# A decoder's second cross attention: the experts' weighing behind the next period's second maximum, the scattered transfers in one group

## The reference, cut to what matters

```python
# cross attention, 16 heads of 16 channels, without a mask
q, k, v = heads(x @ Wq.T + bq), heads(ctx @ Wk.T + bk), heads(ctx @ Wv.T + bv)
probs = softmax(q @ k.T / sqrt(16))
x = layernorm(x + (probs @ v) @ Wo.T + bo)

# routing: 32 experts, 4 for each token, at most C places in each
scores = sigmoid(X @ gate_w.T)
_, idx = top_k(scores + bias, 4)
w = take_along_axis(scores, idx)
w = w / clip(sum(w), 1e-12)
pos = place of this choice among all tokens' choices of the same expert   # a running count
row idx*C + pos of the experts' input = X (dropped where pos >= C)
# later: the expert's output row times w, summed over the 4 choices
```

## Time and profile before

| | us |
|---|---|
| median of 3 runs | 2905.83 |
| lowest and highest | 2905.07, 2911.41 |
| the profiled execution | 2889.48 |
| its span on the core | 2887.5 |
| of it xattn1, about | 2237 to 2684 |
| busy: TensorE, VectorE, ScalarE, GpSimd | 2437.7, 1924.8, 1129.1, 995.1 |
| TensorE's granted clock, mean of the span | 0.92 |

### The profile page before, as it was taken

One profiled execution on the slowest core, in us unless ns is written; L12 is line 12 of the kernel. 1 busy time (PEld: TensorE's weight loads), 2 busy tenths in 40 slices (PEclk: granted clock), 3 DMA queues, 4 the chain that ended last, 5 costly groups with the idle time before them and its releaser, 6 DMA issues. The chain is left out here.

```text
span 2887.5 us, 50682 instructions
## 1 busy us (share of the span) xinstructions
PE 2437.7 (84%) x17441; PEld 2057.2 (71%) x17442; DVE 1924.8 (67%) x5065; ACT 1129.1 (39%) x2063; POOL 995.1 (34%) x1326
## 2 busy tenths in 40 slices
PE   3999996899998699999999999957675988986770
PEld 3878875566665699999999999946563666664770
DVE  7999982576676566666666665556453688786458
ACT  2566552555554222221221212212472655553550
POOL 3555552111111352233321330045111144544664
PEclk8999998999999899999999999978887999886885
DMA  2244103224220200013121120021003334220436
GB/s 70 96 145 144 34 1 74 71 66 122 72 67 16 101 31 29 29 66 112 33 73 61 41 73 29 29 68 56 13 0 75 88 100 131 74 60 3 142 121 242
DMA packets 170627, 206.26 MB, mean 71 GB/s; under 512 B 21062, under 2 KB 148848, under 8 KB 170481
## 3 DMA queue, kind: packets, MB, share of 16 engines
q1 hardware_dynamic: 139680, 154.58, 17.8%
q0 software_dynamic: 15360, 23.63, 2.6%
q10 hardware_dynamic: 15440, 26.22, 2.6%
HBM read 95.42 MB, written 77.20 MB: 60 GB/s over the span
## 5 line engine op out<-in xcount | busy, mean ns | idle before, releaser
L1576 PE MATMUL m_gu<-m_x_hi,m_w_hi 128*128 128x256 f32 x1632 | 463.0, 284 | 18.0 <-issue 10.5
L1576 PE MATMUL m_gu<-m_x_hi,m_w_lo 128*128 128x256 f32 x1632 | 459.2, 281 | 0.0
L1576 PE MATMUL m_gu<-m_x_lo,m_w_hi 128*128 128x256 f32 x1632 | 458.9, 281 | 0.0
L1613 ACT ACTIVATE m_sg<-m_gu 128x256 f32<-128x256 f32 x408 | 156.7, 384 | 672.0 <-PE m_gu L1576 672.0
L1647 DVE TENSOR_TENSOR m_h<-m_sg,m_gu 128x256 f32<-128x256 f32 x408 | 171.7, 421 | 292.0 <-ACT m_sg L1613 289.1
L1106 ACT ACTIVATE x_pt<-x_ps 128x1024 f32<-128x1024 f32 x256 | 262.0, 1024 | 224.5 <-PE x_ps L934 222.7
L1576 PEld LDWEIGHTS m_gu<-m_x_hi,m_w_hi 128*128 128x128 f32 x1632 | 310.5, 190 | 22.4 <-issue 11.9
L1576 PEld LDWEIGHTS m_gu<-m_x_hi,m_w_lo 128*128 128x128 f32 x1632 | 310.6, 190 | 0.0
L1576 PEld LDWEIGHTS m_gu<-m_x_lo,m_w_hi 128*128 128x128 f32 x1632 | 310.5, 190 | 0.0
L1208 DVE CUSTOM_DVE_ANT_0 x_ps<-x_ps,x_mb 128x256 f32<-128x256 f32 x512 | 201.6, 456 | 112.8 <-PE x_ps L934 112.7
L1565 PE MATMUL m_yp<-m_w_hi,m_h_hi 128*128 128x256 f32 x816 | 239.4, 293 | 4.7 <-DVE m_h_lo L1649 4.4
(11 more groups left out here) (320 smaller groups left out, 5640.2 us busy)
## 6 DMA issues: line engine op xcount, KB each, us to landing
yt<-zero SPq DMA_DIRECT2D x8, 2048.0 KB, 10.6
x_qpack<-x_qh SPq DMA_DIRECT2D x128, 128.0 KB
x_kpack<-x_kh SPq DMA_DIRECT2D x128, 128.0 KB
m_yr<-yt SPq DMA_DIRECT2D x16, 1024.0 KB, 13.2
m_x<-xs SPq DMA_DIRECT2D x36, 256.0 KB
ys<-m_y SPq DMA_DIRECT2D x35, 256.0 KB, 2.2
xs<-zero SPq DMA_DIRECT2D x8, 1072.0 KB, 5.8
m_x<-xs SPq DMA_DIRECT2D x32, 268.0 KB
```

Of the source, the lines that this page charges most:

```text
L1576: ins = pe.matmul(gu[:, m % 4, n, :], wp[n][:, c, m * P:m * P + P], xp_[:, c, :], start=(c == 0 and k == 0), stop=(c == KC - 1 and k == 2))
L1613: act.activation(sg[:, m % 4, :], gu[:, m % 4, 0, :], ACT.Silu).then_inc(silu_ready, 1)
```

## The change

In the unmasked cross attention `weigh_experts` of block n moves on VectorE from behind the values of period n+3 to behind the second maximum (number 1) of period n+4, right behind `place` and maximum 1 and ahead of `take_logits`. Its last operation no longer waits for itself but raises a new semaphore, `gate_ready`. On GpSimd the first four transfers of a block move from between the low queries and the low keys to behind the root of the normalization, in front of the other four, and each group waits for `gate_ready` besides `dst_ready`. The masked cross attention keeps its order.

```diff
@@ -859,6 +859,7 @@
             def slots_out(n, t):
                 pool.wait_ge(dst_ready, n + 1)
+                pool.wait_ge(gate_ready, n + 1)
                 pool.sem_inc(st.pool_passed, 1)
...
@@ -870,12 +871,11 @@
             for p in PERIODS:
                 at(p + 1, low_queries)
-                if not masked:
-                    at(p - 4, slots_out, 0)
                 at(p + 1, low_keys)
                 at(p - 2, add_bias)
                 at(p - 2, rstd_of)
                 if not masked:
+                    at(p - 4, slots_out, 0)
                     at(p - 4, slots_out, 1)
...
@@ -1290,8 +1290,8 @@
-                    s.do(dve.tensor_tensor(st.rows1[:, blocks(n), D + 2 * K1:ROW1], gt[:],
-                                           tmp[:, :, 1:2].to_broadcast([P, TB, topk]), ALU.mult))
+                    dve.tensor_tensor(st.rows1[:, blocks(n), D + 2 * K1:ROW1], gt[:],
+                                      tmp[:, :, 1:2].to_broadcast([P, TB, topk]), ALU.mult).then_inc(gate_ready, 1)
...
@@ -1319,6 +1319,8 @@
                 at(q, maxima, 0)
                 at(r - 1, place)
                 at(q, maxima, 1)
+                if not masked:
+                    at(r - 1, weigh_experts)
                 at(r, take_logits)
                 at(q, maxima, 2)
                 at(r, choose)
@@ -1328,7 +1330,8 @@
                 at(r, one_hot)
                 at(q, maxima, 5)
                 at(a, values)
-                at(r, weigh_experts)
+                if masked:
+                    at(r, weigh_experts)
                 at(q, maxima, 6)
```

More of the change, by code:

```diff
@@ L749, in xattn_stage @@
         hit_ready, pos_ready, pos_taken, dst_ready = sem("hit_ready"), sem("pos_ready"), sem("pos_taken"), sem("dst_ready")
-        sent = sem("rows_sent")
+        sent, gate_ready = sem("rows_sent"), sem("gate_ready")
         d_steps = sem("dve_steps")
```

## The result

The changed kernel took **2944.38 us** (median of 4 runs, 2940.91 to 2946.15), the kernel before beside it 2907.53 (4 runs): a ratio of **1.0129, 95% interval 1.0107 to 1.015**. The forecast was 2873.0 with a range up to 2895: wrong, and on the wrong side.

The account below looks back on a forecast made before the run. TensorE was busy 84% of the span; in the second cross attention, collisions beside transfers (1.50 us a period) and a lower clock (16.3 us) cost time. Terms summed to -32.8 us from the 2905.83 median: 2873.0, range 2858 to 2895.

Parts of the forecast that it names:

- the eight in a row: GpSimd's eight transfers behind the root: low queries 2.9 us late, add at 1255 over before them, cost nothing, margin 0.5 us.
- Collisions: Cast and counts no longer collide with late low keys and bias add: 1.48 us in each of eleven periods, -16.5 us.
- Weighing off the path: Weighing no longer delays the seventh maximum on VectorE: 0.8 us in each of thirteen periods, -10.4 us.
- its new place: Weighing behind the second maximum makes VectorE up to 0.72 us late; 0.25 taken twelve times, +3.0 us.
- The clock: Shorter waits before the eighth scores keep TensorE's granted clock at 1.00 in periods 4 to 13, -16.3 us.
- The loads of the next stage: In period 8 late packing of the keys behind these loads gives that period's gain back, +2.3 us.
- The tail: At the stage's end 24 transfers instead of twenty stand behind the last normalization on GpSimd, +5.1 us.
- The base: Difference taken from the 2905.83 us median, not the profiled 2889.48; the 16 us gap may mean more low clock.
- Rival 1: TensorE's clock does not recover, so the 16.3 us are not won: 2889.3 us, chance 0.18.
- rival 2: GpSimd's bias add starts before the last one-hot add and holds it, losing 6.5 us: 2879.5 us, chance 0.11.
- Rival 3: Low queries, late by one more stall, push the low keys back over the cast: 2905.8 us, no change, chance 0.05.
- Rival 4: VectorE stretches the transfers in GpSimd's queue before the low queries to 2.0 us each: slower, 2938 us, chance 0.04.

Follow-up runs that it names:

- y1: The changed kernel without further edit, measured again in a group with TensorE's signals on time: 2886.29 us, ratio 0.9973 to the kernel before.
- z1: The changed kernel without further edit, in another group with signals on time: 2884.72 us, ratio 0.9975 to the kernel before.
- y4: The changed kernel with four transfers ahead of the normalization's root and four behind it, signals on time: 2857.76 us, ratio 0.9876 to the kernel before.
- x1: The changed kernel with the first four transfers back at their old place, signals on time: 2859.56 us, ratio 0.9875 to the kernel before.
- z4: The changed kernel with four transfers ahead of the root, four behind, and weighing at its old place, signals late: 2893.01 us, ratio 0.9957.
- x2: The changed kernel with the weighing back at its old place, signals on time: 2888.28 us, ratio 0.9992 to the kernel before.
- w1: The changed kernel with four transfers ahead of the root and four behind it, signals late: 2879.77 us, ratio 0.9918 to the kernel before.
- z2: The kernel before, unedited, in a group with signals late: 2906.68 us, ratio 1.0002 to the kernel before.
- w2: The changed kernel with all transfer rows but those to slot 0 out of bounds, signals late: 2946.81 us, ratio 1.0149 to the kernel before.

## Why the prediction was wrong

Its sum was built on a profile taken with signals on time, so I hold it against the *on time* groups first, then say what the *late* ones add. There the change gave -7.4 us (y1) and -6.6 (z1), where -32.8 was forecast; in the *late* group of the result it gave +36.9. In both kinds of group the same term of the sum failed, the eight in a row put at nothing, but by two mechanisms.

- **Collisions, -16.5: right only together with the next term.** Cast 0.16 and count 0.18 us as drawn, low keys and bias add beside maxima. A full-clock period fell from 24.73 to 22.46 us in y4, by the 1.50 + 0.77 of the two terms. But they are not prices of two separate moves: the weighing alone (x1, 23.02) already gave 1.71 of these 2.27 us and the clock, with the collisions still there. Once the weighing is gone the collisions cost 0.56 us, and x1 is as fast as y4.
- **Weighing off the path, -10.4, and its new place, +3.0: right, the second too careful.** Period 3 fell by 0.77 us. 0.64 of it is the move; the other 0.13 stands in z4 and x2 too, which keep the old place, and their only other difference on VectorE is the signal in place of the last operation's wait for itself. In y4 periods with transfers took 22.5 us, no more than period 3: the new place cost nothing.
- **"What the eight in a row push on GpSimd: cost nothing, margin 0.5 us": this step failed.** The row's length (10.1 us) and the low queries' lateness (2.9) were right. I asked whether the low queries would meet the add at 1255, saw it end over 0.5 us ahead of their start, and took that for enough. It was not: right behind a transfer they hold an add that starts 0.65 us ahead of them until they are done. A margin of 0.5 us became 1.8 us in a period, 14.1 of the 18.4 between y1 and y4. The mechanism was one that the prediction had used two paragraphs earlier for the low keys. The Trainium skill (SBUF — State Buffer, Who interferes with whom) says of an instruction of VectorE with two SBUF inputs that it "contends with a GpSimd instruction that reads SBUF"; the subtraction of the low queries is one and agrees, the scattered transfer held none of 782. How a subtraction holds what started ahead of it, no run here shows. In the result itself, 2944.38 us, the same term failed in another way: beside eight in a row TensorE's signals came late, and periods 4 to 13 took 305.21 us, where four and four in another *late* group (w1) took 260.42.
- **The clock, -16.3: right in its mechanism where the margin holds.** 0.99 and 231.82 us in y4 against the forecast of "near 229", 0.97 and 250.18 in the change, since the maximum that comes 1.8 us later leaves a new thin stretch: in y1 TensorE was busy 1.02 of the 3 us from 2362 at 1.00, and the next 3 us had 0.59.
- **The loads of the next stage, +2.3.** Mis-sized: the period that has them took 28.3 us in y4 where 22.7 + 2.3 = 25.0 was meant; nearly all of before's 28.9 stays. The other nine, at 22.6 on average, made up 0.8 us of it.
- **The tail, +5.1: right.** From the end of the last root to the last transfer 28.26 us before, 33.5 in y1.
- **The base.** I took the difference from 2905.83 and put the 16 us between the profiled execution and the median down to more low clock. The late signals are likely the larger part: z2, the same kernel in a *late* group, has a span of 2901.8 us, 14.3 over that of the profile. This stage is 11.3 longer in it and the next, moe1, 5.2, while what lies ahead is 2.2 shorter; the 5.2 come in groups on time too (y4).

**The rivals.** Rival 1 (the clock stays low) and rival 2 (bias add) did not come true; y4 had the clock and no race. Rival 3 named the low queries pushed back by the row, but over the cast. Rival 4, the slower one, had the right place, GpSimd's queue before the low queries, and the wrong mechanism: no transfer was stretched (973 ns in the middle, at most 1188), VectorE's instructions were held instead. So the sentence of the Trainium skill (SBUF — State Buffer, SBUF: two separate sides) on 620 ns growing to 3100 finds no support in this case.

**What the late signals add.** Between z2 and the changed kernel, both *late*, the spans differ by 42.5 us: 36.5 in periods 4 to 13 (268.67 to 305.21), 5.2 in the tail, the rest small and of both signs. No row of the profile that the prediction read showed this. I could have asked why all three timed runs lay 16 us or more above the profiled one.

**What stays open.** What in a group makes signals late is not known: not the chip's number, not the rows, not the packing. How transfers issued by GpSimd hold TensorE's signals, whether it is the signals or the matmuls' true ends, and at which length between four and eight the waits grow so long, was not settled. Whether the 5 to 6 us by which moe1 varies between runs (from the last transfer to the end of the span 207.0 in the profile before, 212.2 in z2, but 212.9 in y4 too) has to do with it was not tried.

**The better version.** Four transfers ahead of the root, four behind it, the weighing moved: 0.9876 with signals on time, 0.9918 with late ones. x1, the weighing alone, is as fast on time (0.9875); it was not run late.

## What to carry to other kernels

When a queue is moved so that something comes later, look also at the operations that start shortly ahead of the late instruction: here one that began 0.65 us earlier was held until it was done. A margin of half a microsecond is no margin. And a sum of terms read from one timeline need not price its moves one by one: run each move alone, for here one of the two brought the whole gain. Where signals can come late, issue scattered transfers from GpSimd in groups of four with other work or a pause between them, and put each group where that queue waits anyway. And when the timed runs stand 16 us apart from the profiled one, take a profile of such a run before building a sum on the other.

## What the runs showed of the hardware that I had not expected

- In four of seven groups TensorE's signals came late beside GpSimd's issuing: waits up to 6.2 us with eight in a row, up to 3.4 (w1) and 4.6 (z4) with four, in the same kernel that had none in another group. The Trainium skill (SBUF — State Buffer, Who interferes with whom) says, of the ports of SBUF, that "PE and ACT never wait on anyone". The matmuls ahead of the stall did take their usual 1.07 and 1.08 us, but their consumers waited 4.80 and 4.45 us for them.
- The stall mostly ends with the row: in w2 ScalarE's copy starts 0.08 us behind the eighth transfer, in the change 0.04. Of the ten such waits of the change in periods 4 to 13, seven end within 0.13 us of an eighth transfer's end, the others 1.1 to 1.7 us behind a transfer.
- A stall of some 5 us sends the granted clock to 0.50, and TensorE then takes 0.80 us for four scores in place of 0.50.
- A subtraction of GpSimd directly behind a scattered transfer holds a small two-input add that starts 0.65 us ahead of it: 2.04 us for 0.23. The transfer alone holds none of 782 such instructions.
- A transfer does hold VectorE's small one-input operations from SBUF to SBUF (lines 1253 and 1313) in its second half: of 107 that started 0.5 to 0.7 us into one, 105 were held until it ended (0.33 to 0.45 us for 0.17 to 0.20); of 174 that started earlier in it, none.
